# Attention heads' outputs: divided and split in their PSUM bank, transposed by DMA instead of on TensorE

## The chip, the cores and the metric

The kernel runs on one core of one Trainium2 chip. The metric is the device time of one execution in microseconds (us). Three runs of the kernel before gave 1673.41, 1673.66 and 1678.37 us, median 1673.66.

## The reference

One transformer layer in float32 on x of 16 x 512 x 128 (batch, tokens, width):

```python
h  = layernorm(x)                                  # eps 1e-5
a  = causal_attention(h, Wq, Wk, Wv)               # 16 heads of 64
y  = layernorm(h + concat(a) @ Wo, eps=1e-3) * gamma + beta
x1 = x + y
h2 = layernorm(x1)
w  = softmax over the 8 largest of h2 @ gate_w.T   # 32 experts
out = x1 + sum_e w_e * (silu(h2 @ gate_e.T) * (h2 @ up_e.T)) @ down_e.T
```

The names are abridged. What matters here is `concat(a) @ Wo`: each head's output (512 tokens x 64) is divided by its softmax denominator, and the outputs of all heads are multiplied with Wo. For that product the heads' outputs must lie with the 128 columns of a pair of heads on the partitions, that is, transposed.

## The kernel before

float32 accuracy is reached with float16 products: each operand is split in an upper half (rounded to float16) and a lower half (what is left, rounded), and a product is three matmuls (`product`: hi x hi, hi x lo, lo x hi). The function `layer` holds one program per engine. Five of the eight PSUM banks (V, G, U, R0, R1) are handed round among all work; two (S0, S1) hold scores, and one (XB) the second half of the layer.

A batch (512 tokens in 4 chunks of 128, C = 4) goes through these steps, and three batches are in work at once: heads of batch n, projections of n + 1, experts of n - 1.

- Projections: `project` and `values` on TensorE, `qk_high`/`v_high` on ScalarE (ACT), `qk_low`/`v_low` on VectorE (DVE). `place_qk` (SyncE, SP) copies keys and queries to where the scores read them, 6 transfers per pair of heads.
- Row maxima: `max_scores` on TensorE, `row_maximum` on DVE, `split_maxima` on GpSimd (POOL), `turn_maxima` on TensorE, `copy_maxima` on ACT, `place_max` on SP.
- Per head: `scores` (TensorE, three parts), `exps` and `p_high` (ACT), `p_low` (POOL), then `times_v` (TensorE), which leaves in one bank four blocks of 64 columns of output and one column of denominators (`pv_bank`).
- `denominators` (L1133) takes the reciprocal on DVE, `divide` (L1140) multiplies the 128 x 256 outputs with it from PSUM into the SBUF tile `o32` (called `o` in the profile's rows).
- Per pair of heads: `turn_heads` transposes the four float32 128 x 128 blocks of `o32` on TensorE (L402, against the identity) into another bank. `o_high` (ACT, L785) copies that bank, 128 x 512, to the upper half of `oT`; `o_low` (DVE, L1145) subtracts for the lower half.
- Per four heads: `times_wo` multiplies `oT` with Wo, `add_heads` (DVE) adds to `y0`.
- Then the two normalizations, routing (`take_logits`, `choose`, `mark_chosen`, `weigh` on DVE, `route` on ACT, `turn_weights` on TensorE), and 16 pairs of experts: `gate_product`, `up_product`, `down_product` on TensorE, `gate_tanh` and `unit_high` on ACT, `gate_times_tanh` and `times_up` on DVE, `weigh_unit` and `unit_low` on POOL, `spread_weights` on SP (one transfer per pair of experts, into a ring of 4).

The order of the work is written out by hand for each engine: lists of calls for the first two batches, a loop `for n in range(2, B - 2)` (12 passes, one batch each), and lists for the last two. Each engine goes through its list in order and waits on counting semaphores. SP's list is in order too: a wait in it holds every later transfer. A bank's next user on TensorE waits (`take`) until the last reader named by the previous user is done; for `times_v` that is the `divide` (`o32_done`).

Of the kernel before, what the change touches and what calls it, by code (L numbers as in the profile page):

```python
# [11 lines left out]
P = 128  # L12
# [3 lines left out]
C = S // P  # L16
# [33 lines left out]
def layer(nc, x, wq, wk, wv, wo, gamma, beta, gate, gate_up, down, ident_c, mask_c,  # L50
          key_rows_c, query_rows_c, tail_c, out):
    with ExitStack() as ctx:
# [18 lines left out]
        def home_of(m, q):  # L71
# [51 lines left out]
        rden = sb("rden", [P, 2, C], F32)  # L123
        o32 = sb("o32", [P, 2, C, 2 * E], F32)
# [8 lines left out]
        logits, dropped, shifted, ex = (  # L133
            sb(name, [P, C, NE], F32) for name in ("logits", "dropped", "shifted", "ex"))
        comb = sb("comb", [P, NE, C], F32)
# [108 lines left out]
        oT_mm, oT_hi, oT_lo, y_mm, y0_done = sem("oT_mm"), sem("oT_hi"), sem("oT_lo"), sem("y_mm"), sem("y0_done")  # L244
# [33 lines left out]
        def _(sp):  # L278
# [71 lines left out]
            place_qk(0, 0); fill_rows(0); fill_rows(1); fill_rows(2); place_qk(0, 1); fill_rows(3); load_x(1)  # L350
            place_max(0, 0); load_xb(0); place_qk(0, 2); place_qk(0, 3); place_qk(0, 4); place_max(0, 1); place_qk(0, 5)
            place_qk(0, 6); fill_rows(4); place_max(0, 2); load_x(2); place_qk(0, 7); place_qk(1, 0); place_max(0, 3)
            load_x(3); place_qk(1, 1); place_max(1, 0); place_qk(1, 2); place_qk(1, 3); place_max(1, 1); place_qk(1, 4)
            load_xb(1); place_qk(1, 5); place_max(1, 2); place_qk(1, 6); keep_weights(0); spread_weights(0, 0)
            spread_weights(0, 1); spread_weights(0, 2); spread_weights(0, 3); spread_weights(0, 4); spread_weights(0, 5)
            place_max(1, 3); place_qk(1, 7); spread_weights(0, 6); spread_weights(0, 7); place_qk(2, 0); place_qk(2, 1)
            place_max(2, 0); spread_weights(0, 8); spread_weights(0, 9); place_qk(2, 2); spread_weights(0, 10)
            spread_weights(0, 11); spread_weights(0, 12); place_qk(2, 3); spread_weights(0, 13); spread_weights(0, 14)
            place_qk(2, 4)

            for n in range(2, B - 2):
                place_max(n, 1); spread_weights(n - 2, 15); load_x(n + 2); place_qk(n, 5); place_max(n, 2); load_xb(n)
                place_qk(n, 6); store(n - 2); place_qk(n, 7); keep_weights(n - 1); spread_weights(n - 1, 0)
                spread_weights(n - 1, 1); spread_weights(n - 1, 2); spread_weights(n - 1, 3); spread_weights(n - 1, 4)
                place_max(n, 3); spread_weights(n - 1, 5); place_qk(n + 1, 0); spread_weights(n - 1, 6)
                spread_weights(n - 1, 7); place_qk(n + 1, 1); place_qk(n + 1, 2); spread_weights(n - 1, 8)
                place_max(n + 1, 0); spread_weights(n - 1, 9); spread_weights(n - 1, 10); spread_weights(n - 1, 11)
                place_qk(n + 1, 3); spread_weights(n - 1, 12); spread_weights(n - 1, 13); spread_weights(n - 1, 14)
                place_qk(n + 1, 4)

            place_max(14, 1); spread_weights(12, 15); place_max(14, 2); place_qk(14, 5); store(12); place_qk(14, 6)
            keep_weights(13); load_xb(14); spread_weights(13, 0); spread_weights(13, 1); spread_weights(13, 2)
            spread_weights(13, 3); spread_weights(13, 4); place_max(14, 3); spread_weights(13, 5); place_qk(14, 7)
            spread_weights(13, 6); place_qk(15, 0); place_max(15, 0); spread_weights(13, 7); spread_weights(13, 8)
            place_qk(15, 1); spread_weights(13, 9); spread_weights(13, 10); place_qk(15, 2); place_qk(15, 3)
# [15 lines left out]
        def _(pe):  # L391
# [1231 lines left out]
```

## Time and profile before

| | |
|---|---|
| median of three runs | 1673.66 us |
| profiled execution | 1674.17 us |
| its span | 1672.4 us |
| TensorE (PE) busy | 1601.0 us, 96% |
| VectorE (DVE) busy | 1414.9 us, 85% |
| ScalarE (ACT) busy | 1399.7 us, 84% |
| GpSimd (POOL) busy | 1410.6 us, 84% |
| DMA, share of 16 engines' span | 52.5% |
| mean granted TensorE clock | 0.991 |

Busy time is the time in which an engine has an instruction in work. On PE the instructions overlap and their ends are modelled, so that its busy share says less than the distance from one start to the next. PEld is PE's weight load, which runs beside the products. A wait is the idle time of an engine and what ended it; "issue" is idle time for which the profile shows no cause. SPq is the queue of SP, which only issues DMAs.

### The profile page before, as it was taken

Reading aid. Unit: us, or ns where it says so; the run is one execution under the profiler, and the core shown is the slowest. Engines: PE = TensorE matmul, PEld = TensorE weight load, DVE = VectorE, ACT = ScalarE, POOL = GpSimd, SP = SyncE. Lnnn points to the kernel's source line nnn. Section 1 sums busy time; section 2 is a strip of 40 time slices with the busy share of each in tenths; the row PEclk is TensorE's granted clock in tenths of the full one; section 3 lists DMA queues with packets and bytes.
Section 4 is the critical chain, followed back from the end, with each engine's and each line's share of the span. In section 5 each row is a group of like instructions: output and inputs, shape, how many; then the busy total and the mean of one; then the engine's idle time right before and its main releaser. Section 6 shows DMA issues by size and latency. Waiting matters only on the chain.

```text
span 1672.4 us, 56372 instructions
## 1 busy us (share of the span) xinstructions
PE 1601.0 (96%) x21209; PEld 1102.9 (66%) x21209; DVE 1414.9 (85%) x4461; ACT 1399.7 (84%) x2371; POOL 1410.6 (84%) x1183
## 2 busy tenths in 40 slices
PE   4799999999999999999999999999999999999968
PEld 1476776767667676676767667676776767666645
DVE  7889789898888989889898988989888898888645
ACT  3999898888989888888988989888898888888742
POOL 0687998979899797998979899797989979799874
PEclk8999999999999999999999999999999999999989
DMA  8655656556554564646446454654645456354523
GB/s 244 153 132 120 147 116 166 136 123 159 128 145 125 137 163 110 167 99 155 132 128 168 118 152 111 157 145 117 163 117 153 131 128 161 88 133 117 133 83 109
DMA packets 213902, 228.55 MB, mean 137 GB/s; under 512 B 20480, under 2 KB 178432, under 8 KB 213376
## 3 DMA queue, kind: packets, MB, share of 16 engines
q1 hardware_dynamic: 213632, 224.94, 52.5%
q8 instruction: 170, 2.79, 0.7%
q14 instruction: 100, 0.82, 0.2%
HBM read 84.89 MB, written 5.24 MB: 54 GB/s over the span
## 4 chain that ended last, share of the span: by engine, by line
PE 76%; POOL 8%; ACT 7%; issue 4%; DVE 2%; DMA 2%; SPq 0%; ACTq 0%; DVEq 0%; POOLq 0%
PE bank_r L393 19%; PE bank_s L393 15%; PE bank_u L393 12%; PE bank_x L393 10%; PE bank_v L393 9%; PE bank_g L393 7%; POOL p_lo L1484 3%; POOL expert_room L1499 2%; ACT p_hi L785 1%; POOL halves L1508 1%; ACT bank_x L804 1%; DMA expert_room<-comb_rows 1%; ACT y L804 1%; PE bank_g L402 1%; PE bank_v L402 1%
## 5 line engine op out<-in xcount | busy, mean ns | idle before, releaser
L1484 POOL TENSOR_TENSOR p_lo<-p,p_hi 128x1280 f16<-128x1280 f32 x256 | 671.3, 2625 | 135.6 <-ACT p_hi L785 135.1
L852 ACT ACTIVATE p<-bank_s,back 128x512 f32<-128x512 f32 (+1 forms) x768 | 462.6, 615 | 72.5 <-PE bank_s L393 53.4
L393 PE MATMUL bank_s<-score_ops 128*128 128x62 f16 (+10 forms) x4096 | 409.1, 232 | 3.7 <-ACT p L852 2.1
L393 PEld LDWEIGHTS bank_s<-score_ops 128*128 128x128 f16 x4096 | 285.2, 97 | 167.5 <-ACT p L852 19.0
L785 ACT ACTIVATE p_hi<-p 128x1280 f16<-128x1280 f32 x256 | 324.7, 1269 | 4.2 <-PE bank_r L393 1.7
L1499 POOL TENSOR_TENSOR expert_room<-expert_room 128x512 f32<-128x512 f32 x240 | 305.4, 1276 | 12.2 <-DMA expert_room<-comb_rows 10.4
L1508 POOL TENSOR_TENSOR halves<-expert_room,halves 128x512 f16<-128x512 f32 x240 | 277.7, 1164 | 0.5
L1127 DVE CUSTOM_DVE_ANT_0 max_junk<-bank_r,mask 128x384 f16<-128x384 f32 (+3 forms) x414 | 188.8, 489 | 18.8 <-PE bank_u L393 9.4
L393 PE MATMUL bank_x<-w_hi,halves 128*128 128x128 f16 x1920 | 197.7, 219 | 4.4 <-POOL halves L1508 4.3
L785 ACT ACTIVATE halves<-expert_room 128x512 f16<-128x512 f32 x240 | 151.0, 630 | 51.1 <-POOL expert_room L1499 34.2
L393 PE MATMUL bank_x<-w_lo,halves 128*128 128x128 f16 x960 | 172.3, 219 | 0.0
L393 PEld LDWEIGHTS bank_x<-w_hi,halves 128*128 128x128 f16 x1920 | 154.5, 98 | 18.2 <-POOL halves L1508 6.4
L393 PE MATMUL bank_r<-tanh_room,w_hi 128*128 128x512 f16 x412 | 123.5, 381 | 0.4 <-DVE rowmax L1127 0.4
L1110 DVE TENSOR_TENSOR nat<-bank_r,nat 128x512 f16<-128x512 f32 x137 | 93.8, 685 | 12.6 <-ACT nat L785 12.6
L1127 DVE CUSTOM_DVE_ANT_0 max_junk<-bank_u,mask 128x256 f16<-128x256 f32 (+3 forms) x238 | 98.8, 449 | 1.3 <-PE bank_g L393 0.8
L393 PEld LDWEIGHTS bank_x<-w_lo,halves 128*128 128x128 f16 x960 | 93.7, 98 | 7.5
L785 ACT ACTIVATE nat<-bank_r 128x512 f16<-128x512 f32 x137 | 81.7, 596 | 18.6 <-PE bank_r L393 17.4
L1127 DVE CUSTOM_DVE_ANT_0 max_junk<-bank_v,mask 128x512 f16<-128x512 f32 (+3 forms) x190 | 95.0, 523 | 1.7 <-PE bank_u L393 0.5
L889 ACT ACTIVATE tanh_room<-bank_g,back 128x512 f32<-128x512 f32 x109 | 75.4, 692 | 24.3 <-PE bank_g L393 22.9
L1127 DVE CUSTOM_DVE_ANT_0 max_junk<-bank_g,mask 128x128 f16<-128x128 f32 (+3 forms) x182 | 84.0, 490 | 6.6 <-PE bank_v L393 6.5
L393 PE MATMUL bank_r<-hT,w_hi 128*128 128x512 f16 x274 | 83.5, 387 | 6.1 <-DVE hT L1105 4.5
L1227 DVE SCALAR_TENSOR_TENSOR expert_room<-bank_r,expert_room 128x512 f32<-128x512 f32 x104 | 71.1, 684 | 18.6 <-PE bank_r L393 17.3
(282 smaller groups left out, 5009.9 us busy)
## 6 DMA issues: line engine op xcount, KB each, us to landing
score_ops<-nat SPq DMA_DIRECT2D x256, 256.0 KB, 3.9
score_ops<-nat SPq DMA_DIRECT2D x512, 128.0 KB, 3.8
expert_room<-comb_rows SPq DMA_DIRECT2D x240, 256.0 KB, 3.4
xt<-in_x SPq DMA_DIRECT2D x16, 256.0 KB, 3.4
xb<-in_x SPq DMA_DIRECT2D x16, 256.0 KB, 3.2
out_y<-expert_room SPq DMA_DIRECT2D x16, 256.0 KB, 3.8
score_ops<-comb_rows SPq DMA_DIRECT2D x16, 256.0 KB, 4.7
expert_room<-in_gate_up SPq DMA_DIRECT2D x1, 2048.0 KB, 10.1
```

Source lines behind the costliest of these rows:

```text
L393: return pe.matmul(dst, lhsT, rhs, start=start, stop=stop, skip_group_check=shared)
L402: last = pe.transpose(dst[:, c * P:c * P + P], src[:, c, :], ident32[:, :])
L785: return act.activation(dst, src, ACT.Copy)
L804: act.activation(dst[:, c, :], src[:, c, :], ACT.Identity, bias=shift[:, which, c:c + 1], scale=rstd[:, which, c:c + 1]).then_inc(ln_out[w ...
L852: act.activation(p32[:, h % P_SLOTS, at:at + cols], bank[score_bank(h, u)][:, 0:cols], ACT.Exp, scale=back[:, SC_SCORE:SC_SCORE + 1]).then ...
L889: act.activation(th, bank[b][:, :], ACT.Tanh, scale=back[:, SC_HALF:SC_HALF + 1]).then_inc(th_done, 1)
L1110: dve.tensor_tensor(nat[:, home_of(m, q), (K_LO, Q_LO)[w], :], bank[b][:, :], nat[:, home_of(m, q), (K_HI, Q_HI)[w], :], ALU.subtract).the ...
L1127: done = dve.tensor_tensor_reduce(max_junk[:, k % 2, at:at + cols], bank[b][:, at:at + cols], mask[:, S - cols:S], 1.0, NEG, ALU.add, ALU. ...
L1227: dve.scalar_tensor_tensor(unit(p, j), bank[b][:, :], UNIT_SHIFT, unit(p, j), ALU.mult, ALU.mult).then_inc(su_done, 1)
L1484: pool.tensor_tensor(p_lo[:, slot, :], p32[:, slot, :], p_hi[:, slot, :], ALU.subtract).then_inc(p_lo_done, 1)
L1499: pool.tensor_tensor(weighed(p, j), weighed(p, j), unit(p, j), ALU.mult).then_inc(a32_done, 1)
L1508: pool.tensor_tensor(a_lo[:, j % 2, :], weighed(p, j), a_hi[:, j % 2, :], ALU.subtract).then_inc(a_lo_done, 1)
```

## The change

- `divide` writes its product back into the same PSUM bank instead of into `o32`. `rden` has four buffers instead of two.
- A new `split_high` on ACT copies the 128 x 256 outputs of one head from the bank to a float16 tile `o_split` in SBUF; a new `split_low` on DVE takes the lower half from the bank. The bank is free for its next user after `split_low` (`o_lo_done`). These are two instructions per head in place of two per pair (`o_high`, `o_low`).
- `turn_heads` is gone. A new `turn_out` on SP sends two transposing transfers per pair, one for the upper halves and one for the lower, from `o_split` (128 x 512 float16) into `oT`. `times_wo` waits for them (`oT_turned`), and `split_high` waits before it writes `o_split` again.
- In routing, `ex` now lies on `shifted` and `comb` on `dropped`; the wait for `combT_mm` moves from `weigh` to `mark_chosen`.
- The lists of all five engines and the banks in them are written anew. Work and count of the other calls are as before.

```diff
-        rden = sb("rden", [P, 2, C], F32)
-        o32 = sb("o32", [P, 2, C, 2 * E], F32)
+        rden = sb("rden", [P, 4, C], F32)
+        o_split = sb("o_split", [P, 2, 2, C, 2 * E], F16)
...
+            def turn_out(m, q):
+                pair = m * PAIRS + q
+                sp.wait_ge(o_hi_done, 2 * pair + 2)
+                wait(sp, y_mm, m * QUADS + q // 2)
+                sp.dma_start(oT[:, q % 2, 0:1].rearrange("p a (c t) -> p (a c) t", c=C), o_split[:, q % 2, 0:1].rearrange("p a c d -> p (a c d)"),
+                             transpose=True).then_inc(oT_turned[q % 2], 16)
+                sp.wait_ge(o_lo_done, 2 * pair + 2)
+                sp.dma_start(oT[:, q % 2, 1:2].rearrange("p a (c t) -> p (a c) t", c=C), o_split[:, q % 2, 1:2].rearrange("p a c d -> p (a c d)"),
+                             transpose=True).then_inc(oT_turned[q % 2], 16)
...
             def times_v(m, h, b):
                 slot = h % P_SLOTS
-                take(b, o32_done, m * H + h + 1)
+                take(b, o_lo_done, m * H + h + 1)
...
-            def turn_heads(m, q, b):
-                take(b, oT_lo, m * PAIRS + q + 1)
-                pe.wait_ge(o32_done, m * H + 2 * q + 2)
-                turn32(bank[b], o32[:, q % 2]).then_inc(oT_mm, 1)
-
             def times_wo(m, g, b):
                 take(b, y0_done, m * QUADS + g + 1)
-                pe.wait_ge(oT_lo, m * PAIRS + 2 * g + 2)
+                for k in range(2):
+                    pe.wait_ge(oT_turned[k], 32 * (m * QUADS + g + 1))
...
-            def o_high(m, q, b):
-                act.wait_ge(oT_mm, m * PAIRS + q + 1)
-                wait(act, y_mm, m * QUADS + q // 2)
-                copy(oT[:, q % 2, 0, :], bank[b][:, :]).then_inc(oT_hi, 1)
+            def split_high(m, h, b):
+                q, ab = h // 2, h % 2
+                act.wait_ge(o32_done, m * H + h + 1)
+                if ab == 0:
+                    wait(act, oT_turned[q % 2], 32 * ((m * PAIRS + q) // 2))
+                copy(o_split[:, q % 2, 0, :, E * ab:E * ab + E], pv_bank(b)[:, :, 0:E]).then_inc(o_hi_done, 1)
...
             def divide(m, h, b):
+                dve.wait_ge(rden_done, m * H + h + 1)
+                heads = pv_bank(b)[:, :, 0:E]
+                dve.tensor_tensor(heads, heads, rden[:, h % 4, :].rearrange("p (c a) -> p c a", a=1).to_broadcast([P, C, E]),
+                                  ALU.mult).then_inc(o32_done, 1)
+
+            def split_low(m, h, b):
                 q, ab = h // 2, h % 2
-                dve.wait_ge(rden_done, m * H + h + 1)
-                if ab == 0:
-                    wait(dve, oT_mm, m * PAIRS + q - 1)
-                dve.tensor_tensor(o32[:, q % 2, :, E * ab:E * ab + E], pv_bank(b)[:, :, 0:E],
-                                  rden[:, h % 2, :].rearrange("p (c a) -> p c a", a=1).to_broadcast([P, C, E]), ALU.mult).then_inc(o32_done, 1)
-
-            def o_low(m, q, b):
-                dve.wait_ge(oT_hi, m * PAIRS + q + 1)
-                dve.tensor_tensor(oT[:, q % 2, 1, :], bank[b][:, :], oT[:, q % 2, 0, :], ALU.subtract).then_inc(oT_lo, 1)
+                dve.wait_ge(o_hi_done, m * H + h + 1)
+                dve.tensor_tensor(o_split[:, q % 2, 1, :, E * ab:E * ab + E], pv_bank(b)[:, :, 0:E],
+                                  o_split[:, q % 2, 0, :, E * ab:E * ab + E], ALU.subtract).then_inc(o_lo_done, 1)
...
             def mark_chosen(p):
                 wait(dve, drop_done, C * p)
+                wait(dve, combT_mm, p)
```

The head of SP's loop before and after, as an example of the lists:

```diff
-                place_max(n, 1); spread_weights(n - 2, 15); load_x(n + 2); place_qk(n, 5); place_max(n, 2); load_xb(n)
-                place_qk(n, 6); store(n - 2); place_qk(n, 7); keep_weights(n - 1); spread_weights(n - 1, 0)
...
+                place_max(n, 1); load_x(n + 2); spread_weights(n - 2, 15); place_qk(n, 5); turn_out(n, 0)
+                turn_out(n, 1); place_max(n, 2); place_qk(n, 6); load_xb(n); turn_out(n, 2); store(n - 2)
+                turn_out(n, 3); place_qk(n, 7); keep_weights(n - 1); spread_weights(n - 1, 0); spread_weights(n - 1, 1)
...
```

## Rows read from the trace of the kernel before

**Rows 1.** The page: busy time by engine, and the chain by engine.
```profile
PE 1601.0 (96%) x21209; PEld 1102.9 (66%) x21209; DVE 1414.9 (85%) x4461; ACT 1399.7 (84%) x2371; POOL 1410.6 (84%) x1183
...
PE 76%; POOL 8%; ACT 7%; issue 4%; DVE 2%; DMA 2%; SPq 0%; ACTq 0%; DVEq 0%; POOLq 0%
```

**Rows 2.** Busy time in a stretch: start:end, length, engines, clock, DMA share, GB/s.
```profile
499.00:1291.00 792.00, 783.48 (x10554) 544.41 (x10553) 691.84 (x2196) 691.42 (x1178) 702.52 (x586) 1.00 0.53 137
```

**Rows 3.** Timeline of SP: start, duration; load_x in two passes that follow each other.
```profile
525.05 0.59 SPq L299 DMA_DIRECT2D xt<-in_x  x1
...
624.53 0.59 SPq L299 DMA_DIRECT2D xt<-in_x  x1
```

**Rows 4.** Waits of PE and PEld, 499 to 1291 us: total, times, longest.
```profile
PE bank_r L393 <- issue: 3.8, 8, 0.5
PE bank_u L393 <- DVE expert_room L1222: 2.6, 8, 0.3
...
PEld bank_r L393 <- issue: 12.8, 39, 0.6
PEld bank_s L393 <- ACT p L852: 8.0, 32, 0.3
```

**Rows 5.** Transposes of o on PE: one form of four, and one turn_heads in the timeline.
```profile
L402 PE MATMUL bank_v<-ident,o x172: 272/273/327, 81.9 to 1498.3; 128*128 128x128 f32 x172
...
600.88 0.60 PE L402 MATMUL bank_g<-ident,o 128*128 128x128 f32 x4
601.31 0.38 PE L393 MATMUL bank_s<-score_ops 128*128 128x512 f16 x1
```

**Rows 6.** Groups by form on ACT: count | busy us, mean ns | idle before.
```profile
L785 ACT ACTIVATE p_hi<-p 128x1280 f16<-128x1280 f32 x256 | 324.7, 1269 | 4.2 <-PE bank_r L393 1.7 <-PE bank_g L393 1.0
L852 ACT ACTIVATE p<-bank_s,back 128x256 f32<-128x256 f32 x256 | 121.4, 474 | 17.8 <-PE bank_s L393 15.7
L785 ACT ACTIVATE nat<-bank_r 128x512 f16<-128x512 f32 x137 | 81.7, 596 | 18.6 <-PE bank_r L393 17.4
L785 ACT ACTIVATE oT<-bank_v 128x512 f16<-128x512 f32 x43 | 25.8, 600 | 0.2 <-PE bank_v L402 0.2
```

**Rows 7.** DVE: o_low and divide by form, and the gamma product within PSUM (min/median/max ns).
```profile
L1145 DVE TENSOR_TENSOR oT<-bank_v,oT 128x512 f16<-128x512 f32 x43 | 29.4, 684 | 0.0
L1140 DVE TENSOR_TENSOR o<-bank_v,rden 128x256 f32<-128x256 f32 x74 | 31.2, 422 | 1.8
...
L1163 DVE TENSOR_TENSOR bank_x<-bank_x,gam x16: 672/676/699, 137.2 to 1620.8; 128x512 f32<-128x512 f32 x16
```

**Rows 8.** Waits of POOL, 499 to 1291 us.
```profile
POOL p_lo L1484 <- ACT p_hi L785: 73.7, 32, 4.8
POOL expert_room L1499 <- DMA expert_room<-comb_rows: 1.1, 2, 0.6
```

**Rows 9.** Waits of SP's queue, 499 to 1291 us.
```profile
SPq L340 <- POOL halves L1508: 127.2, 57, 5.6
SPq L312 <- DVE nat L1110: 111.6, 32, 9.2
SPq L324 <- ACT rowmaxT L785: 65.7, 20, 5.8
SPq L332 <- ACT expert_room L785: 27.3, 8, 3.8
SPq L303 <- DVE x L1166: 14.5, 8, 1.9
```

**Rows 10.** Issues of one line of place_qk (128 KB each): duration ns min/median/max, landing.
```profile
L316 SPq DMA_DIRECT2D score_ops<-nat x256: 607/628/2043, 21.4 to 1570.1; - x128
...
DMA to landing us min/median/max: 3.0/3.8/7.7
```

**Rows 11.** The page: DMA queue of SP: packets, MB, share of 16 engines.
```profile
q1 hardware_dynamic: 213632, 224.94, 52.5%
```

**Rows 12.** Timeline: the two copies of the turn_heads of rows 5.
```profile
603.12 0.59 ACT L785 ACTIVATE oT<-bank_g 128x512 f16<-128x512 f32 x1
...
604.46 0.68 DVE L1145 TENSOR_TENSOR oT<-bank_g,oT 128x512 f16<-128x512 f32 x1
```

**Rows 13.** Last turn_heads and times_wo in the timeline; then two pieces of the chain.
```profile
1609.42 0.63 PE L402 MATMUL bank_u<-ident,o 128*128 128x128 f32 x4
...
1612.46 0.22 PE L393 MATMUL bank_r<-w_hi,oT 128*128 128x128 f16 x1
...
1616.19 1.16 POOL halves L1508
1617.35 0.20 POOL var_eps L1447
```

More of the change, by code:

```diff
@@ L132, in layer @@
         a_hi, a_lo = halves[:, 0], halves[:, 1]
-        logits, dropped, shifted, ex = (
-            sb(name, [P, C, NE], F32) for name in ("logits", "dropped", "shifted", "ex"))
-        comb = sb("comb", [P, NE, C], F32)
+        logits, dropped, shifted = (
+            sb(name, [P, C, NE], F32) for name in ("logits", "dropped", "shifted"))
+        ex = shifted
+        comb = dropped[:, :, :].rearrange("p c e -> p (c e)").rearrange("p (e c) -> p e c", c=C)
         top8 = sb("top8", [P, C, TOPK], F32)
@@ L243, in layer @@
         pv_mm, rden_done, o32_done = sem("pv_mm"), sem("rden_done"), sem("o32_done")
-        oT_mm, oT_hi, oT_lo, y_mm, y0_done = sem("oT_mm"), sem("oT_hi"), sem("oT_lo"), sem("y_mm"), sem("y0_done")
+        o_hi_done, o_lo_done, y_mm, y0_done = sem("o_hi_done"), sem("o_lo_done"), sem("y_mm"), sem("y0_done")
+        oT_turned = [sem(f"oT_turned{k}") for k in range(2)]
         yg_done, x1_done = sem("yg_done"), sem("x1_done")
@@ L354, in _ @@
[L354 to L358, printed above, removed]
@@ L371, in _ @@
[L371 to L375, printed above, removed]
@@ new lines, in _ @@
+            place_qk(1, 1); load_x(3); place_max(1, 0); turn_out(0, 5); place_qk(1, 2); turn_out(0, 6); turn_out(0, 7)
+            place_max(1, 1); place_qk(1, 3); place_qk(1, 4); turn_out(1, 0); load_xb(1); place_qk(1, 5); turn_out(1, 1)
+            place_max(1, 2); keep_weights(0); spread_weights(0, 0); spread_weights(0, 1); place_qk(1, 6)
+            spread_weights(0, 2); place_qk(1, 7); turn_out(1, 2); spread_weights(0, 3); spread_weights(0, 4)
+            place_max(1, 3); turn_out(1, 3); spread_weights(0, 5); spread_weights(0, 6); place_qk(2, 0)
@@ new lines, in _ @@
+            place_max(15, 0); place_qk(15, 2); turn_out(14, 6); spread_weights(13, 9); turn_out(14, 7)
+            spread_weights(13, 10); spread_weights(13, 11); spread_weights(13, 12); spread_weights(13, 13)
+            place_qk(15, 3); place_max(15, 1); spread_weights(13, 14); spread_weights(13, 15); place_qk(15, 4)
+            place_qk(15, 5); turn_out(15, 0); turn_out(15, 1); place_max(15, 2); place_qk(15, 6); turn_out(15, 2)
+            store(13); load_xb(15); keep_weights(14); spread_weights(14, 0); spread_weights(14, 1)
@@ new lines, in _ @@
+            denominators(1, 3, U); divide(1, 3, U); split_low(1, 2, R0); h2_low(0); qk_low(1, 13, V); split_low(1, 3, U)
+            take_logits(0); v_low(1, 7, G); choose(0); denominators(1, 4, R0); gate_times_tanh(0, 0, V); mark_chosen(0)
+            qk_low(1, 14, R1); gate_times_tanh(0, 1, G); weigh(0); times_up(0, 0, U); divide(1, 4, R0)
+            add_heads(1, 0, G); split_low(1, 4, R0); qk_low(1, 15, V); denominators(1, 5, R1)
+            row_maximum(1, 3, 0, 0, R0); divide(1, 5, R1); row_maximum(1, 3, 0, 1, G); row_maximum(1, 3, 1, 0, V)
@@ new lines, in _ @@
+            split_low(14, 4, U); row_maximum(14, 3, 0, 0, R0); h_low(15, G); denominators(14, 5, R1)
+            row_maximum(14, 3, 0, 1, V); divide(14, 5, R1); row_maximum(14, 3, 1, 0, R0); row_maximum(14, 3, 1, 1, G)
+            split_low(14, 5, R1); add_heads(14, 0, U); h2_low(13); row_maximum(14, 3, 2, 0, R0)
+            row_maximum(14, 3, 2, 1, V); denominators(14, 6, R1); take_logits(13); divide(14, 6, R1); choose(13)
+            mark_chosen(13); gate_times_tanh(13, 0, G); denominators(14, 7, R0); weigh(13); v_low(15, 0, V)
@@ new lines, in _ @@
+            take_logits(14); choose(14); mark_chosen(14); weigh(14); row_maximum(15, 3, 2, 0, R1)
+            gate_times_tanh(14, 0, R0); row_maximum(15, 3, 2, 1, U); denominators(15, 7, G); divide(15, 7, G)
+            times_up(14, 0, R0); gate_times_tanh(14, 1, R1); split_low(15, 6, V); times_up(14, 1, U)
+            row_maximum(15, 3, 3, 0, R0); split_low(15, 7, G); row_maximum(15, 3, 3, 1, V); row_maximum(15, 3, 4, 0, R0)
+            row_maximum(15, 3, 4, 1, U); gate_times_tanh(14, 2, G); denominators(15, 8, V); divide(15, 8, V)
```

1130 lines of the change are left out of this document (568 added, 562 removed).

## The prediction

> **What bounds the kernel now.** I read the page's busy shares and chain first, then one long steady stretch by engine, then the waits of each engine in that stretch. The page [rows 1] shows PE busy 96% of the span and carrying 76% of the chain that ended last. Steady state is a loop with one batch per pass: the same load of x is issued at 525.05 and at 624.53 us, so a pass takes 99.5 us [rows 3], and the 792 us of [rows 2] hold 7.96 passes. Per pass, ACT, DVE and POOL work 86.9, 86.9 and 88.3 us (691.4, 691.8 and 702.5 divided by 7.96). PE shows 98.4 us, but its ends are modelled. I take PE's own work from its waits: in the stretch PE waits 8.5 us (4 rows, of which the two largest stand) and its weight loads 68.8 us (16 rows), of which 35.5 is "issue", leaving 33.3 for named engines [rows 4]. So PE waits between 4.2 us (33.3/7.96) and 9.7 us (77.3/7.96) of a pass; I take 5.8, nearer the lower end because a weight load that waits often does so behind a running matmul. PE's own work is then 93.7 us (bounds 89.8 to 95.3). PE is first, with the other three only 5 to 7 us behind. That is the picture the whole forecast rests on: there is one fully loaded engine and three that will catch up with it soon.
>
> **The change, part by part.**
>
> *TensorE loses the heads' transposes.* There are 8 turn_heads per batch with 4 fp32 transposes each. Each lasts 273 ns by its row, yet four start at 600.88 and the next product starts at 601.31: 0.43 us for four in the pipe [rows 5]. A pass saves 8 x 0.43 = 3.4 us, the run 128 x 0.43 = 55 us. Nothing replaces them on PE.
> The Trainium skill (TensorE: Matmul & The Clock Gate, Part 4: PE-mode transpose) gives some 275 ns for a 128x128 transpose inside a kernel. By that the run would save 512 x 0.275 = 141 us; the row's duration agrees with it, its spacing doesn't, and I go by spacing.
>
> *ACT.* 8 copies of 512 columns at 0.600 us go (4.8 us per pass). 16 split_high of 256 columns (4 blocks of 64) come. Two lines bound such a copy: Copy takes 1.269 us at 1280 columns and 0.596 at 512 [rows 6], 0.88 ns a column, so 0.37 at 256; the Exp of 256 columns takes 0.474. I take 0.39, nearer the Copy line. That is 6.2 us, net +1.4 (bounds +1.1 to +2.8): ACT 88.3.
>
> *DVE.* 8 o_low at 0.684 go (5.5 us). 16 split_low come, the same kind of instruction at 256 columns; the divide of that size takes 0.422 [rows 7], so 6.8 us, net +1.3: DVE 88.2. The divide itself now writes PSUM. The gamma product that reads and writes PSUM takes 0.676 at 512 columns, no more than o_low into SBUF [rows 7], so I charge nothing; if PSUM-to-PSUM were to cost a tenth more it would be 0.7 us a pass. The denominators are unchanged.
>
> *POOL.* The same instructions in a new order: 88.3. Its only large wait is for p_hi of ACT, 9.3 us a pass (73.7/7.96) [rows 8], so it too has room of 10% at today's period.
>
> *SP and the DMA engines.* 16 transposing transfers of 128 KB come per pass. No row shows one. SP now waits 364 us of the 792 (8 rows; those of 14 us and more stand) [rows 9], 45.8 us of a pass, and is occupied 53.7. A plain 128 KB issue holds it 0.63 us and lands after 3.8 us [rows 9, 10]. The longest issue of that line held it 2.04 us [rows 10]. Bounds: 0.63 to 2.04 per transfer, 10 to 33 us a pass. I take 1.2, since a transfer that is cut into blocks should cost more to issue than a plain one, which is a choice between the ends and not read anywhere. SP is then occupied 73 us of some 97, and its slack falls from 46 to 24 us. This hides only because the DMAs behind it are early: POOL waited 1.1 us in the whole stretch for spread weights [rows 8]. Moved past: each turn_out waits first for o_hi_done and y_mm, then for o_lo_done, and behind it stand place_qk, place_max, spread_weights. place_max is the tight one, as the PE list reaches the scores of the next quad soon after it. The DMA queue is 52.5% busy [rows 11]; 16 x 128 KB on the 13.6 MB of a pass (137 GB/s x 99.5 us) adds 15% of that, 8 points. Landing latency of oT is hidden: times_wo stands several heads later in the list, except in the last batch.
> The Trainium skill is of two minds: Advanced Engine Details and Errata, X-Bar Transpose (TRN2), says transposing DMAs go as fast as regular ones, by which the hold would be near the plain row; VectorE: DVE Perf Modes, The three transpose paths, gives 1309 ns for one 128x128 bf16 block, by which four blocks take 5.2 us. No row here shows either.
>
> *PSUM banks.* A turn_heads held its bank from 600.88 until o_low ended at 605.14, 4.3 us [rows 5, 12]; 8 of these go, 34 us of the 5 x 99.5 = 498 bank-us. Each of the 16 times_v now keeps its bank through two more hops; the old pair shows what they are: from the transposes' end (601.48) to the end of o_low, 3.7 us, and with 256 columns 0.5 less. At 2 to 3.2 us each that is 32 to 51 us more. Net -2 to +17 bank-us, up to 3.4% of all: about neutral.
>
> *Small edits.* rden of four instead of two buffers, comb on dropped's room, ex on shifted's: the wait moved into mark_chosen is for combT_mm of the batch before, a pass old. 0, and at most some tenths in a pass if a routing chain came late. The wait on oT_turned in split_high stands at the head of ACT's queue; exps and p_high are behind it, and PE and POOL behind those. It asks for the pair two before, so it costs nothing as long as SP is less than about four heads (25 us) late.
>
> *Ends.* The last batch has no cover: its last turn_heads (1609.42), ACT and DVE copy take 3.0 us to the products with oT at 1612.46 [rows 13]. With hops through SP and a landing of 3.8 us that becomes some 7, of which up to 1.5 us hide behind POOL, which frees the residual statistics only at 1617.35 [rows 13]. I charge +2 us.
>
> **Sum.** PE's work falls from 93.7 to 90.3 us a pass; the others come up to 88.2 to 88.3. Today the pass is 5.8 us over its most loaded engine. With four engines within 2 us of each other, each in a fixed order, the in-order queues collide more often; I take 6.9 over, so 97.2 us a pass, 2.3 us less. From 202 us to about 1590 the kernel runs 14 passes: -32 us; the pass before them, still without experts for much of it, -2; the end +2. The profiled run of 1674.2 us (span 1672.4) becomes 1642; the median of 1673.66 stands 0.5 under the profiled run, so 1642 serves for both.
>
> **Rivals.**
> 1. *The whole relief arrives*: PE's overhang stays 5.8 us and the banks get freer. 3.4 x 16 = 55, less 2 at the end: 1621. For it: the chain is 76% PE. Against: the other three were 6 us behind and are now 2.
> 2. *The gain is lost to balance*: overhang grows by the whole 3.4 us (to 9.2). The pass stays at 99.5 and the time at 1674. For it: ACT and DVE both gain 1.3 us, and every head now needs ACT and DVE one after another before its bank is free.
> 3. *Slower through the banks*: PE waits for banks more. Its weight loads wait 4.2 us a pass for named engines today [rows 4]. It decides from the point where these waits grow by 3.4 us a pass; were they to grow by 4.9 (a little over double), a pass takes 101.0 and the run 1674 + 16 x 1.5 = 1698.
> 4. *Slower through SP*: a hold h per transposing transfer. SP's 46 us of waits are eaten up at h = 2.9 us (46/16); from there a pass is 53.7 + 16h. At 3.5 us it is 109.7 and the run 1674 + 16 x 10.2 = 1837. Even at 2 us the slack is 14 us, and a late place_max, not fullness, would stop the scores; priced at 2 us for each of 4 place_max, less the relief, +4.6 a pass: 1748. Against: the longest plain issue is 2.04. By the Trainium skill's figure (VectorE: DVE Perf Modes, as above), an estimate, h would be 5.2 and a pass 137 us, some 2270 us in all.
> 5. *It doesn't do what it says*: the transposes leave PE by the list, so this can't be, save that a transfer in two-byte pieces is so slow that times_wo waits. That is rival 4 seen from PE.
>
> **Chances.** Forecast 0.48, full relief 0.14, lost to balance 0.15, banks 0.12, SP 0.11. The forecast's own range is 1628 to 1660 (overhang 5.9 to 8.1 us). For 8 in 10: rival 1's upper half belongs in, so 1617 at the low end; above, rival 2 and most of rival 3, 1698. 0.3% of 1673.7 is 5 us, about what a measurement of this kernel can tell from no change. Faster: the forecast's 0.48, rival 1's 0.14 and 0.04 of rival 2: 0.66. Same: the other 0.11 of rival 2. Slower: rivals 3 and 4, 0.23. Outside the range lie SP's 0.11, a third of rival 3 (0.04) and some 0.04 below.
>
> **What would show it.** Right: a pass of 97 us between loads of x; no fp32 transposes of o on PE; PE busy still above 95% and 75% or more of the chain; split_high near 0.39 us, split_low near 0.42, divide still 0.42; SP's hold per transposing transfer 0.6 to 2 us; POOL's wait for p_hi below 9 us a pass. Wrong: a hold above 2.9 us; weight loads that wait for DVE o or ACT for over 7 us a pass; POOL or PE waiting for comb_rows, rowmaxT or nat transfers by more than 2 us a pass; times_wo waiting for oT.

## The result, and the profile after

| | before | after |
|---|---|---|
| median | 1674.71 us (4 runs) | 1694.49 us (1692.26 to 1695.71, 4 runs) |
| span of the profiled run | 1672.4 us | 1693.9 us |
| ratio to before | | 1.0113, interval 1.0093 to 1.0133 |

The change makes the kernel 1.1% slower; 1642 us was forecast. In the experiments below one run of plain_four (1935.65 us) and one of max_act (3454.14 us) fell in a far slower state and are left out of the times. The page after has two lines that answer to [rows 1] and one to [rows 11]; the line of DMA packets is new.

```profile
PE 1575.2 (93%) x20697; PEld 1051.0 (62%) x20697; DVE 1432.9 (85%) x4589; ACT 1409.9 (83%) x2499; POOL 1413.1 (83%) x1183
...
DMA packets 353165, 262.09 MB, mean 155 GB/s; under 512 B 159744, under 2 KB 317696, under 8 KB 352640
...
q1 hardware_dynamic: 352896, 258.53, 67.7%
...
PE 51%; SPq 12%; POOL 11%; DMA 8%; issue 7%; ACT 6%; DVE 5%; ACTq 0%; POOLq 0%; DVEq 0%
```

TensorE has less to do (96% busy before) and carries less of the chain: 51% in place of 76%. SP's queue, 0% before, now has 12% of it, and the DMAs 8% (2% before). The same stretch as in [rows 2], and SP's loads of x as in [rows 3], the second one here eight passes after the first:

```profile
499.00:1291.00 792.00, 763.94 (x10262) 512.25 (x10261) 695.39 (x2254) 691.61 (x1236) 700.73 (x588) 1.00 0.70 158
```
```profile
539.20 0.41 SPq L301 DMA_DIRECT2D xt<-in_x  x1
...
1337.40 0.42 SPq L301 DMA_DIRECT2D xt<-in_x  x1
```

A pass takes (1337.40 - 539.20)/8 = 99.8 us, as long as before (99.5); 97.2 was forecast. The load at 539.20 already stands 14 us behind that of [rows 3]. So the first batches lose time, and in the loop all that TensorE was spared is used up.

POOL's wait for ACT and the waits of the engines for DMAs, 499 to 1291 us (total, times, longest), which answer to [rows 4, 8]; then three of SP's own waits, as [rows 9]:

```profile
POOL p_lo L1519 <- ACT p_hi L790: 24.9, 25, 2.3
...
POOL expert_room L1534 <- DMA expert_room<-comb_rows: 23.2, 13, 3.9
POOL xb L1523 <- DMA xb<-in_x: 19.7, 8, 3.1
...
PE bank_s L412 <- DMA score_ops<-rowmaxT: 8.9, 8, 2.7
...
PE bank_u L412 <- DMA oT<-o_split: 4.8, 5, 1.8
```
```profile
SPq L314 <- DVE nat L1133: 65.7, 9, 8.3
SPq L352 <- POOL halves L1543: 54.7, 36, 4.9
...
SPq L326 <- ACT rowmaxT L790: 15.8, 16, 1.5
```

Before, the only transfer of these that came late was comb_rows, by 1.1 us [rows 8]. Now experts' weights, x for the residual, maxima and turned heads come late, all of them transfers of SP. Once sent, they take little longer than before: the expert weights land after a median of 3.7 us, 3.4 before. Added up, SP's nine kinds of waits are 186 us of the 792 (364 before): it is occupied (792 - 186)/7.94 = 76 us of a pass, close to the 73 forecast. That is still not full, yet it is late. The timeline of SP (start, duration) shows how:

```profile
610.56 0.62 SPq L352 DMA_DIRECT2D expert_room<-comb_rows  x1
611.28 1.35 SPq L317 DMA_DIRECT2D score_ops<-nat  x1
612.67 0.62 SPq L318 DMA_DIRECT2D score_ops<-nat  x1
...
616.49 1.43 SPq L329 DMA_DIRECT2D score_ops<-rowmaxT  x2
618.02 1.21 SPq L335 DMA_TRANSPOSE oT<-o_split  x1
619.28 1.27 SPq L338 DMA_TRANSPOSE oT<-o_split  x1
620.60 2.27 SPq L352 DMA_DIRECT2D expert_room<-comb_rows  x2
...
628.86 1.23 SPq L335 DMA_TRANSPOSE oT<-o_split  x1
630.13 1.26 SPq L338 DMA_TRANSPOSE oT<-o_split  x1
```

From 611.28 to 631.4 us no gap is longer than 0.1 us: 20 us of transfers in a row, each sent when its turn comes and not when its data are ready. They are part of a longer unbroken stretch in the same trace: 49 transfers from 593.4 to 639.2 us with no gap over 0.15 us. Six passes running, from 593 us on, have such an unbroken stretch of 45 to 48 us; before, the longest is 10.7 us. Over a third of SP's 186 us of waiting is before place_qk, for keys not yet made (65.7 us, up to 8.3 at once); then it runs behind. The transposing transfers over the whole run (ns min/median/max), with their landing (us):

```profile
L335 SPq DMA_TRANSPOSE oT<-o_split x128: 1189/1237/2379, 79.2 to 1629.6; - x128
L338 SPq DMA_TRANSPOSE oT<-o_split x128: 1188/1266/2697, 81.4 to 1630.8; - x128
...
DMA to landing us min/median/max: 2.4/3.2/6.3
```

### The profile page after: what moved, and what is told of

It is laid out like the page before. It is cut to its first block, busy times and chain, and to the rows that moved or that the text cites. A ratio compares the mean times of both kernels' runs of the same rounds, so it can differ in the third digit from the quotient of the medians.

```text
span 1693.9 us, 55734 instructions
## 1 busy us (share of the span) xinstructions
PE 1575.2 (93%) x20697; PEld 1051.0 (62%) x20697; DVE 1432.9 (85%) x4589; ACT 1409.9 (83%) x2499; POOL 1413.1 (83%) x1183
## 2 busy tenths in 40 slices
DMA packets 353165, 262.09 MB, mean 155 GB/s; under 512 B 159744, under 2 KB 317696, under 8 KB 352640
## 3 DMA queue, kind: packets, MB, share of 16 engines
q1 hardware_dynamic: 352896, 258.53, 67.7%
## 4 chain that ended last, share of the span: by engine, by line
PE 51%; SPq 12%; POOL 11%; DMA 8%; issue 7%; ACT 6%; DVE 5%; ACTq 0%; POOLq 0%; DVEq 0%
PE bank_r L412 13%; PE bank_s L412 10%; PE bank_u L412 7%; PE bank_x L412 7%; PE bank_v L412 7%; PE bank_g L412 6%; POOL halves L1543 4%; POOL expert_room L1534 3%; POOL p_lo L1519 3%; SPq L319 3%; SPq L318 3%; DMA oT<-o_split 3%; SPq L317 2%; DMA expert_room<-comb_rows 2%; SPq L335 2%
## 5 line engine op out<-in xcount | busy, mean ns | idle before, releaser
L1150 DVE CUSTOM_DVE_ANT_0 max_junk<-bank_r,mask 128x128 f16<-128x128 f32 (+3 forms) x499 | 216.2, 469 | 5.9 <-PE bank_g L412 1.7
L412 PE MATMUL bank_r<-tanh_room,w_hi 128*128 128x512 f16 x386 | 116.2, 383 | 0.3
L412 PE MATMUL bank_r<-nat 64*128 64x384 f16 (+3 forms) x499 | 93.1, 299 | 15.2 <-DVE v_lo L1138 6.5
L412 PEld LDWEIGHTS bank_x<-w_lo,halves 128*128 128x128 f16 x960 | 94.6, 99 | 10.7
L1150 DVE CUSTOM_DVE_ANT_0 max_junk<-bank_v,mask 128x128 f16<-128x128 f32 (+3 forms) x157 | 75.5, 506 | 27.1 <-PE bank_g L412 20.5
L899 ACT ACTIVATE tanh_room<-bank_r,back 128x512 f32<-128x512 f32 x113 | 77.8, 688 | 18.8 <-PE bank_r L412 13.3
L1150 DVE CUSTOM_DVE_ANT_0 max_junk<-bank_u,mask 128x384 f16<-128x384 f32 (+3 forms) x189 | 90.0, 501 | 3.8 <-PE bank_r L412 3.5
L1133 DVE TENSOR_TENSOR nat<-bank_r,nat 128x512 f16<-128x512 f32 x110 | 75.3, 684 | 14.1 <-ACT nat L790 14.1
L412 PE MATMUL bank_v<-v_hi,p_lo 128*128 128x65 f16 x850 | 86.5, 194 | 0.0
L790 ACT ACTIVATE nat<-bank_r 128x512 f16<-128x512 f32 x110 | 66.4, 604 | 24.1 <-PE bank_r L412 21.6
L412 PE MATMUL bank_v<-v_lo,p_hi 128*128 128x64 f16 x850 | 86.4, 193 | 0.0
```

The source lines that it names most:

```text
L412: return pe.matmul(dst, lhsT, rhs, start=start, stop=stop, skip_group_check=shared)
L790: return act.activation(dst, src, ACT.Copy)
L899: act.activation(th, bank[b][:, :], ACT.Tanh, scale=back[:, SC_HALF:SC_HALF + 1]).then_inc(th_done, 1)
L1133: dve.tensor_tensor(nat[:, home_of(m, q), (K_LO, Q_LO)[w], :], bank[b][:, :], nat[:, home_of(m, q), (K_HI, Q_HI)[w], :], ALU.subtract).the ...
L1150: done = dve.tensor_tensor_reduce(max_junk[:, k % 2, at:at + cols], bank[b][:, at:at + cols], mask[:, S - cols:S], 1.0, NEG, ALU.add, ALU. ...
```

## The experiments

"Hold" is how long a transfer keeps SP, "SP's time" is the sum of the durations of all SP transfers that start in 499 to 1291 us, added up from the trace, and "unbroken" is the longest stretch (us) of SP's transfers there with no gap over 0.15 us. Theories: S, SP's in-order queue is late and costs the time; X, the small packets of the transposing transfers on the DMA engines do; B, four engines in balance, so that time taken off TensorE is worth nothing; L, the new lists. Each comparison is with the kernel before on the same chip.

| kernel | us | ratio, interval | SP's time | unbroken | pass |
|---|---|---|---|---|---|
| before | 1674.7 to 1676.3 | 1 | 404.5 | 10.7 | 99.6 |
| plain_one | 1645.94 | 0.9823 (0.9808, 0.9837) | 461.6 | 8.9 | 97.0 |
| plain_two | 1644.39 | 0.9806 (0.9787, 0.9825) | 507.2 | 23.2 | 97.0 |
| one_turn | 1649.62 | 0.9846 (0.9829, 0.9863) | 523.3 | 23.0 | 97.1 |
| one_held | 1655.04 | 0.9875 (0.9861, 0.989) | 564.0 | 32.6 | 97.3 |
| plain_four | 1681.69 | 1.0026 (1.0008, 1.0043) | 584.4 | 46.7 | 99.6 |
| after | 1694.49 | 1.0113 (1.0093, 1.0133) | 595.4 | 47.7 | 99.8 |
| merged_rows | 1724.61 | 1.028 (1.025, 1.0309) | 622.0 | 50.1 | 101.8 |
| quad_turn | 1698.38 | 1.0139 (1.0122, 1.0156) | 503.5 | 15.9 | 98.7 |
| held_old | 1727.73 | 1.0315 (1.0295, 1.0334) | 549.8 | 30.2 | 103.7 |

The pass is the distance of two loads of x, eight passes apart, over 8. From plain_one down to merged_rows, all with the new lists, SP's time orders the kernels' times, save that the two plain ones are alike: from 462 to 507 us it costs nothing, from there to 564 some 5 us at each of the two steps, and from 564 to 622 another 70. quad_turn, one_xb and the kernels that load ACT or TensorE more lie above this curve, for other reasons that follow below.

**Fewer or other transfers.** one_turn:

```diff
-                sp.dma_start(oT[:, q % 2, 0:1]..., o_split[:, q % 2, 0:1]..., transpose=True).then_inc(oT_turned[q % 2], 16)
                 sp.wait_ge(o_lo_done, 2 * pair + 2)
-                sp.dma_start(oT[:, q % 2, 1:2]..., o_split[:, q % 2, 1:2]..., transpose=True).then_inc(oT_turned[q % 2], 16)
+                sp.dma_start(oT[:, q % 2]..., o_split[:, q % 2]..., transpose=True).then_inc(oT_turned[q % 2], 16)
```

plain_one, plain_two and plain_four are the same with one, two or four transfers without `transpose=True` (the heads' outputs stay unturned, so the results are others).

> The changed kernel with one transposing transfer per pair of heads (upper and lower halves together, 128 x 1024) in place of two; both lists as they are. Theory S (SyncE's in-order queue is what ends last: 16 transposing transfers a pass hold it about 1.3 us each, and place_max, load_xb and spread_weights go out late behind them): if the hold is per transfer, SP is relieved of some 8 x 1.2 = 10 us a pass and the kernel comes to about 1675 us; if the hold grows with the size (about 2.4 us for the big one), nothing is relieved, and the upper halves' turn now also waits for the lower ones: about 1695 to 1710. Theory X (what costs is the landing of the small packets, 3.2 us a transfer and the DMA engines at 0.70): the same bytes and packets go, so 1690 to 1700 whatever the hold. Theory B (four engines in balance, the product taken off TensorE is worth nothing): 1690 to 1697. Theory L (the new lists themselves cost it): 1690 to 1697.

> The changed kernel with one plain transfer per pair of heads, not transposing (the heads' outputs go to the output product unturned, so the result is another one; all instructions of the four compute engines are as before). It takes away both the hold of SyncE (0.63 us a plain transfer against 2 x 1.3 us a pair) and the small packets. Theory S: SP relieved of 8 x 2 = 16 us a pass, the passes go under 99.4 us, 1640 to 1665 us in all. Theory X: the same 1640 to 1665. Theory B: 1685 to 1695, since neither SP nor the DMAs mattered. Theory L: 1685 to 1695.

> The changed kernel with two plain transfers per pair (128 x 512 each), not transposing: the same count and bytes as the transposing ones. SP's hold would fall from some 2.6 to 1.3 us a pair, the small packets go. Theory S: half of what plain_one gains, about 1665 to 1680. Theory X: all of what plain_one gains, 1640 to 1665. Theories B and L: 1685 to 1695.

> The changed kernel with four plain transfers per pair (128 x 256 each), not transposing: SP is held for 4 x 0.63 = 2.5 us a pair, as it is by the two transposing ones (2 x 1.3), with few and larger packets on the DMA engines. Theory S: no gain, 1688 to 1700. Theory X: all of plain_one's gain, 1640 to 1665. Theories B and L: 1685 to 1695, which S alone can't be told from here; plain_one tells them apart.

one_turn is 45 us faster than after and 26 faster than before. From its page, its busy time by stretch, and its oT transfers in all:

```profile
DMA packets 349068, 262.06 MB, mean 159 GB/s; under 512 B 155648, under 2 KB 313600, under 8 KB 348544
...
PE 74%; POOL 7%; ACT 6%; DVE 6%; issue 4%; DMA 2%; SPq 0%; DVEq 0%; ACTq 0%; POOLq 0%
```
```profile
499.00:1291.00 792.00, 779.77 (x10567) 527.29 (x10565) 713.92 (x2309) 710.06 (x1268) 721.77 (x604) 1.00 0.71 163
```
```profile
L336 SPq DMA_TRANSPOSE oT<-o_split x128: 1231/1310/2384, 79.0 to 1582.4; - x128
...
DMA to landing us min/median/max: 3.0/3.6/5.5
```

The hold is per transfer: 1.31 us for 128 x 1024 against 1.24 for half of it. The small packets, the bytes and the DMA share (0.71) are as in after (0.70), and the landing is even longer (3.6 against 3.2 us); yet SP is gone from the chain. That is against X. Its waits in the stretch:

```profile
POOL xb L1521 <- DMA xb<-in_x: 18.4, 8, 3.7
PE bank_s L410 <- DMA score_ops<-rowmaxT: 1.2, 2, 0.8
PE bank_u L410 <- DMA oT<-o_split: 0.7, 1, 0.7
POOL expert_room L1532 <- DMA expert_room<-comb_rows: 0.6, 1, 0.6
```

plain_four has no transposing transfer at all and is 37 us slower than plain_two, which moves the same bytes. Its DMA queue is as busy (60.2% against 60.4%) though its packets are smaller; what is left is the 0.60 us for which each of its added transfers holds SP.

```profile
L336 SPq DMA_DIRECT2D oT<-o_split x256: 464/601/2155, 79.1 to 1620.1; - x128
L339 SPq DMA_DIRECT2D oT<-o_split x256: 477/601/1886, 81.5 to 1621.4; - x128
...
DMA to landing us min/median/max: 1.8/2.4/6.6
```

The 13 us by which after is slower than plain_four may be the 11 us more of SP's time, or the transposing; these runs don't tell them apart. B and L fall with one_turn as the whole cause: the lists and the work of the four engines are untouched.

Theory S had the direction right and the sizes wrong. It took the cost for proportional, and plain_two and one_turn came out 21 and 25 us below its figures; plain_two lies in the range of X. plain_four lies 6 us below S's range and 17 above X's.

**A hold alone, in the old and in the new list.** held_old is the kernel before with `hold(4)`, four empty transfers that nothing waits for, at eight places of SP's looped list; one_held is one_turn with `hold(1)` behind each turn_out:

```diff
+            def hold(n):
+                for _ in range(n):
+                    k = spares[0]
+                    wait(sp, spared[k % 4], 16 * (k // 4))
+                    sp.dma_start(spare[:, k % 4], w_hi[:, 0:8]).then_inc(spared[k % 4], 16)
+                    spares[0] += 1
```

> The kernel before with 32 more plain transfers of 2 KB in each of the 12 looped passes, eight times four in SyncE's list, that nobody waits for: at 0.5 to 0.6 us each they hold SP for 16 to 19 us a pass, about as long as the 16 transposing ones in the new kernel do, and move next to nothing. Theory S: the old kernel becomes slower too, 1680 to 1710, though its SP waited 45 us a pass in the trace. If SP's slack hides such holds as the prediction said: 1672 to 1678, and the loss of the new kernel is of its own list.

> one_turn with one more plain transfer of 2 KB behind each of the eight transposing ones in the looped passes, that nobody waits for: 0.6 us x 8 = 4.8 us a pass of SP's time and no bytes. SP's issue time in 499:1291 goes from 523 to some 562 us, between plain_two (507: 1644) and plain_four (584: 1683). Theory S: 1655 to 1675. If the room is used up only nearer to the 595 us of the changed kernel: 1649 to 1655.

```profile
L339 SPq DMA_DIRECT2D spare<-w_hi x384: 478/600/1683, 227.7 to 1467.2; - x192
```
```profile
PE bank_s L408 <- DMA score_ops<-rowmaxT: 15.7, 15, 2.0
...
POOL expert_room L1514 <- DMA expert_room<-comb_rows: 13.9, 9, 2.3
```

The old kernel becomes 51 us slower by 245 us of holds (384 of them, the sum of their durations) that move nearly nothing (DMA share 0.54 against 0.53): 4.1 us a pass for 20.4 us. SP waited 46 us of a pass before. So this idle share hid some 16 of the 20 us and not all, and two of the transfers that came late in after do so here. The loss is 18 us above S's range. one_held shows where it begins in the new list: +5.4 us for 63 us of holds, the intervals just touching.

**SP relieved elsewhere, and bigger transfers.** merged_rows leaves the 16 transposing transfers and joins place_qk's upper rows for both heads (both get rows of the first head, another result); quad_turn sends one 128 x 2048 transposing transfer per two pairs:

```diff
+                for n, k, part in ((0, 4, K_HI), (4, 2, Q_HI)):
+                    here = score_ops[0:E, n:n + k, slot].rearrange("p a b s -> p a (b s)")
+                    both = home[0:E, part:part + 2].rearrange("p (a b) s -> p a (b s)", a=1)
+                    sp.dma_start(here, both.to_broadcast([E, k, 2 * S])).then_inc(placed[q], 16)
```

> The changed kernel with its 16 transposing transfers a pass as they are, but place_qk does its keys' and queries' upper rows for both heads of a pair in one transfer each: 4 transfers a pair in place of 6, the same bytes (both heads then get rows of the first, another result). It relieves SP of 16 x 0.6 = 10 us a pass somewhere else than at the turned outputs. Theory S (it is SP's sum that decides, not the transposing transfers themselves): back to about what one_turn gave, 1645 to 1665. If the transposing transfers' own latency or the crossbar was at fault: 1685 to 1697.

> The changed kernel with one transposing transfer for two pairs (128 x 2048), 4 a pass in place of 16; lists as they are. Theory S with a hold per transfer of some 1.4 us: SP relieved of 15 us a pass, all that one_turn (1649.6) left of it; but the split of a pair then waits until the transfer of two pairs has landed: 1640 to 1660. If the hold grows with the size (it was 1.27 us at 128 x 512 and 1.35 at 128 x 1024) it comes nearer to one_turn or above it.

```profile
L321 SPq DMA_DIRECT2D score_ops<-nat x256: 605/1724/2891, 22.8 to 1627.8; - x128
...
DMA to landing us min/median/max: 3.1/5.3/11.4
```

Two transfers of 0.63 us became one of 1.72 (median of both kinds): merged_rows took nothing off SP but added 27 us of its time, and is 30 us slower. It missed its aim; what it adds is one more point on the curve. So joining transfers isn't free: the transposing one grew from 1.24 to 1.31 us when doubled, and to 2.03 in quad_turn. quad_turn's loop is faster than after's, (1330.31 - 541.01)/8 = 98.7 us a pass. Yet with less of SP's time than one_turn it is 49 us slower than that, far outside its 1640 to 1660. In the written-out batches split_high waited up to 4.6 us for the landing of two pairs, which fits the loss there (6 us behind the loop); what holds its loop at 98.7 wasn't tried.

**The hold on another engine.** In max_act (from after) and one_max (from one_turn) ACT issues place_max's transfers behind its copy of the maxima:

```diff
                 copy(rowmaxT[:, :], bank[b][0:8 * C, 0:P]).then_inc(rowmaxT_ready, 1)
+                wait(act, score_mm, UNITS * 2 * (m * PAIRS + 2 * g + 1 - SLOTS + 1))
...
+                    act.dma_start(home, rowmaxT[16 * k:16 * k + 16, :]).then_inc(max_placed[g], 16)
```

> The changed kernel, with its two transposing transfers per pair, but place_max's two transfers a quad are issued by ScalarE right behind its copy of the maxima, not by SyncE: SP is relieved of 8 x 0.69 = 5.5 us a pass and a transfer that PE waits for no longer stands in its queue; ScalarE (0.87 busy) is held as long. Theory S: 1665 to 1685. Were the transposing transfers themselves at fault (latency, small packets): 1688 to 1700.

> one_turn with place_max issued by ScalarE as in max_act. By theory S SyncE is no longer what ends last in one_turn (0% of its chain), so this relieves a queue that has room: 1642 to 1652, and slower than one_turn (1649.6) if ScalarE's added 5.5 us a pass brings it level with TensorE.

1738.0 us (1.0367) and 1740.5 (1.0387): max_act lies 53 us above theory S's range and 38 above the other, one_max 88 above its range. A wait of ACT in one_max, and the transfers that it issues (ns min/median/max):

```profile
ACT p L867 <- issue: 35.2, 23, 2.1
```
```profile
L860 ACTq DMA_DIRECT2D score_ops<-rowmaxT x61: 621/622/1023, 498.7 to 1273.0; - x61
```

61 transfers hold ACT 0.62 us each, and the exps behind them begin later. That is some 5 us a pass, but one_max loses 6.5 a pass to one_turn ((1378.48 - 550.08)/8 = 103.6); the rest may be the slot that ACT now has to wait for. ScalarE, 87 to 90% busy with work of its own, had no room for what SP does. The Trainium skill (DMA: Bandwidth & Descriptors, Rules for kernel authors) says that spreading DMAs over engines only saves issue time; issue time is what was short here, and even so the spread lost 43 us (max_act) and 91 (one_max).

**What TensorE's relief is worth.** relief_mm and relief_all take work off it in the old order, and with it the turning of the heads, so the results are others; one_work and after_work put 4 x 0.22 us ahead of each times_wo back on it in the new one:

```diff
# relief_mm
-                turn32(bank[b], o32[:, q % 2]).then_inc(oT_mm, 1)
+                mm(bank[b][:, :], ident[:, :], wh(WQ, 0, S), True, True).then_inc(oT_mm, 1)
# one_work, after_work
+                for _ in range(4):
+                    mm(bank[b][:, :], ident[:, :], wh(WQ, 0, S), True, True)
```

> The kernel before with turn_heads taken out and its two copies reading the divided outputs in SBUF instead of the bank (the heads' outputs go to the output product unturned, another result): TensorE is relieved of the four turning products a pair and of their waits, nothing else moves, and SyncE has nothing added. Theory S (the saved time of TensorE is real, the new kernel lost it to SyncE's queue): 14 passes x 3 us or more come off, 1615 to 1640. Theory B (four engines in balance): 1668 to 1676.

> The kernel before with the four turning products of turn_heads (0.43 us a pair) replaced by one f16 product of 512 columns into the same bank (computation changed: the bank then holds columns of the weights, not the turned heads). All reads, copies, waits and queues stay. TensorE is relieved of about half of what the change relieves it of: 8 x 0.2 = 1.7 us a pass. Theory S (time taken off TensorE counts where nothing is added to SyncE): about 16 x 1.7 = 27 us off, 1645 to 1660. Theory B (four engines in balance): 1670 to 1677.

> one_turn with four more f16 products of 512 columns ahead of each times_wo, whose result the product behind them overwrites: 4 x 0.22 = 0.87 us a quad, 3.5 us a pass put back on TensorE, as much as the turned heads took. Theory S with TensorE as the bound in one_turn (74% of its chain): the whole 3.5 x 15 = 52 us come back, some 1700. If the forecast's share holds (2.3 of 3.4): 1649.6 + 36 = 1685. Theory B, as relief_mm gave it in the old order (0.7 of 1.7): some 1671.

> The changed kernel with the same four products ahead of each times_wo. If SyncE's queue has taken TensorE's place, part of the 3.5 us a pass hides in TensorE's new waits: 1700 to 1725, a smaller addition than in one_work. If both count in full, whatever the other does: 1694.5 + 52 = 1746.

relief_all took 1724.75 us (1.0295), outside both expectations, and tested something else: its lower halves are now made from an operand in SBUF, and DVE took 1273 ns on average for what takes 684 from PSUM [rows 7]. Single ones took from 660 to 3005 ns; POOL's p_low grew too (2671 ns against 2625, up to 3090). That looks like DVE and POOL holding each other up, which wasn't tried.

```profile
L1143 DVE TENSOR_TENSOR oT<-o,oT 128x512 f16<-128x512 f32 x128 | 162.9, 1273 | 5.3 <-ACT oT L783 5.1
```
```profile
L1143 DVE TENSOR_TENSOR oT<-o,oT x128: 660/984/3005, 78.5 to 1659.6; 128x512 f16<-128x512 f32 x128
```

relief_mm gave 1664.36 (0.9933): 12 us for some 27, between the two expectations, so in the old order under half of it counts. one_work gave 1697.01 (1.0136), 47.4 us over one_turn for 64 x 0.87 = 56 us of work: in the new order 85% of it counts. after_work gave 1719.39 (1.0276), only 24.9 over after: there over half hides, which fits that SP's queue and the DMAs have taken 16% of the chain. The chains of one_work and after_work:

```profile
PE 83%; DVE 7%; issue 3%; POOL 3%; ACT 2%; DMA 1%; SPq 0%; ACTq 0%; DVEq 0%; POOLq 0%
```
```profile
PE 64%; SPq 9%; DMA 7%; issue 5%; DVE 5%; POOL 5%; ACT 4%; ACTq 0%; POOLq 0%; DVEq 0%
```

**One transfer one place earlier.** one_xb is one_turn with `load_xb(n)` ahead of `place_qk(n, 6)` in the loop.

> one_turn with load_xb(n) one place earlier in the looped list, ahead of place_qk(n, 6). POOL waits 18.4 us in 499:1291 for this load. As TensorE bounds one_turn: no difference, 1647 to 1652. If POOL's late end counts (its 2.3 us a pass): 1625 to 1640.

1664.56 us (0.9934), 15 us slower, which neither theory had. Two lines of its waits, SP's and POOL's:

```profile
SPq L305 <- DVE x L1187: 20.1, 8, 2.5
```
```profile
POOL xb L1521 <- DMA xb<-in_x: 1.5, 1, 1.5
```

POOL's 18.4 us of waits went to 1.5 and bought nothing. But SP now stands 2.5 us a pass before x1, which it didn't in one_turn, and place_qk and all behind it leave later: a pass takes (1312.60 - 527.71)/8 = 98.1 us, 1.0 more. SP's list decides by its order, not only by its sum.

The best version that computes the layer is one_turn, 1.5% faster than the kernel before.

## Why the prediction was wrong

The runs split the result in three steps that add up: before to one_work (all of the change except TensorE's relief and the second transfer) +22.3 us; one_work to one_turn (TensorE's relief) -47.4; one_turn to after (16 transposing transfers in place of 8) +44.9. In sum +19.8. The sizes depend on the order of the steps: with the products added back the second transfer costs 22.4 (one_work to after_work), not 44.9.

- *The failed step is SP's.* The prediction took 1.2 us per transfer (1.24 and 1.27 measured, up to 2.7) and 73 us of occupation (76), and then said that the slack of 24 us hides it "only because the DMAs behind it are early", and let rival 4 decide from 2.9 us. So it had the hold and the sum right and priced SP's lateness at nothing; the second transfer alone cost 44.9 us. The DMAs behind weren't early enough: the 1.1 us of [rows 8] is a wait of one of SP's kinds and says nothing of how much later it may come. held_old shows that the old list didn't have room for all of 20 us either; plain_one, with 0.54 us a pair, sets the price of the holds in after at 1694.5 - 1645.9 = 49 us, the transposing included. The sum of the rest, 1642, is within 8 us of one_turn and 3 of plain_two, in part by luck, as the next item shows. Rival 4 had the right place, and named the late place_max, but put its point of decision (2.9 us, or 2 at the least) too high.
- *TensorE.* 3.4 us a pass off, of which 2.3 were to arrive after an overhang of 1.1: one_work has 47 of 56 us arriving, more than the forecast took, and 22 us of losses elsewhere that it hadn't. The two errors offset each other: the net, 25, is near the 32 forecast, and the pass of one_turn is 97.1 against 97.2.
- *ACT and DVE.* One form each, count | busy, mean ns:

```profile
L790 ACT ACTIVATE o_split<-bank_v 128x256 f16<-128x256 f32 x85 | 32.1, 377 | 0.2 <-DMA oT<-o_split 0.2
```
```profile
L1161 DVE TENSOR_TENSOR bank_v<-bank_v,rden 128x256 f32<-128x256 f32 x85 | 36.6, 430 | 1.9
L1167 DVE TENSOR_TENSOR o_split<-bank_v,o_split 128x256 f16<-128x256 f32 x85 | 35.3, 416 | 2.5 <-ACT o_split L790 2.4
```

  0.38 and 0.42 as forecast (0.39, 0.42); the divide within PSUM costs 8 ns more, 0.1 us a pass.
- *Banks (rival 3).* Weight loads wait 47.9 us for named engines in the stretch, 6.0 a pass in place of 4.2, of which DVE's o_split is 1.3 (6.9 and 3.3 us). The growth of 1.8 is under the 3.4 at which this rival was to decide.
- *DMA engines.* 52.5% became 67.7%, 15 points and not 8: the bytes rose as forecast, but with packets under 512 B, 159,744 in place of 20,480. one_turn has the same, so it costs nothing here. The Trainium skill (Advanced Engine Details and Errata, X-Bar Transpose) says that transposing DMAs are as fast as regular ones. The trace agrees only roughly in the landing, 3.2 us against 3.8 for a plain one of the same bytes [rows 10] and 2.7 for one of the same shape (plain_two), and not in the hold, twice the plain one. The Trainium skill (VectorE: DVE Perf Modes, The three transpose paths) gives 1309 ns for one 128x128 block; an estimate of 5.2 us for four from it agrees with neither the hold nor the landing.
- *Marks named ahead.* The hold stayed under 2.9 us, yet POOL and PE waited 4.0 us a pass for comb_rows and rowmaxT ((23.2 + 8.9)/7.94), over the 2 that were to prove it wrong. POOL's wait for p_hi fell as forecast, to 3.1 us a pass (24.9/7.94).

Open: where the 22 us of the rest lie. one_work's load of x at 534.39 us is 9 behind that of [rows 3], eight passes add 3.4 (100.0 a pass), and 8 come after; new lists, the longer use of the banks and the wider DVE and ACT work weren't separated. Nor was it tried why the old order gives back under half of TensorE's relief and the new one 85%; the added products also stand at another place of the list, ahead of times_wo, and not where the turned heads did.

## What to carry to other kernels

An in-order queue's idle share isn't all slack: it idles where the list waits for data and runs late behind that place. Here the queue was idle for 186 of 792 us and yet sent for 46 us at a stretch. So look at the longest unbroken stretch of transfers and at what waits at its end, or test added holds with empty transfers before the change is built. Before a change puts work on such a queue, count its transfers, for the hold goes by the transfer more than by its bytes; join those with the same waits and measure the hold again, since it can grow too (two of 0.63 us became one of 1.72).

## What the runs showed of the hardware

- A transposing SBUF-to-SBUF transfer of f16 held SP 1.24 us at 128 x 512 (after), 1.31 at 128 x 1024 (one_turn) and 2.03 at 128 x 2048 (quad_turn), and landed after 3.2, 3.6 and 4.5 us; a plain one of 128 x 512 held it 0.55 to 0.60 and landed after 2.7 (plain_two).
- A plain transfer of 2 KB in 128 rows (held_old) held SP as long as one of 128 KB: 0.60 us.
- A subtraction of 128 x 512 on DVE with its fp32 operand in SBUF, beside a busy POOL, took 660 to 3005 ns, 1273 on average (relief_all); with that operand in PSUM 684 (before).
- Four fp32 transposes of 273 ns each cost TensorE 0.43 us [rows 5]; f16 products of 512 columns started 0.22 us apart (one_work).
